# Product-key layers: batch norm's chain moved into layer norm's programs, and four small loads moved ahead

## The reference, cut to what matters

```python
x = x + _L0_ffn_ref(_layernorm(x, axis=-1), gamma, beta, w_q, keys, key_in, key_out)

def _L0_ffn_ref(inputs, gamma, beta, w_q, keys, key_in, key_out):
    x = inputs.reshape(b * n, d)
    mu = jnp.mean(x, axis=0)
    var = jnp.mean(jnp.square(x - mu), axis=0)
    xn = (x - mu) * jax.lax.rsqrt(var + BN_EPS) * gamma + beta
    q = (xn @ w_q.T)...
    sim = jnp.einsum('pbnhd,hkpd->pbnhk', q, keys)
    ...
    o = jnp.einsum('bnd,bnhkd->bnhk', inputs, w_down)
    o = gelu(o) * softmax(scores)
    return jnp.einsum('bnhk,bnhkd->bnd', o, w_up)
```

## Time and profile before

| what | value |
|---|---|
| median of 3 runs | 3775.61 us (3774.59 to 3777.11) |
| the profiled execution's own time | 3767.38 us |
| its span (first to last instruction) | 3765.6 us |
| PE busy | 3243.5 us, 86% |
| DVE busy | 2937.1 us, 78% |
| ACT, POOL busy | 1575.8 us, 42%; 672.2 us, 18% |
| TensorE clock granted, mean | 0.933 of full |
| DMA, mean over the span | 55 GB/s |

### The profile page before, as it was taken

The page is one execution under the profiler, slowest core; times in us unless marked ns, Lnnn a source line. Parts: engine busy times, 40 slices in busy tenths (PEclk is TensorE's granted clock), DMA queues, the critical chain, the costliest instruction groups (busy, mean ns, idle before and its releaser), DMA issues. The chain is left out here.

```text
span 3765.6 us, 81247 instructions
## 1 busy us (share of the span) xinstructions
PE 3243.5 (86%) x29418; PEld 2264.2 (60%) x29418; DVE 2937.1 (78%) x8854; ACT 1575.8 (42%) x2148; POOL 672.2 (18%) x308
## 2 busy tenths in 40 slices
PE   3997579999999985659999999998379999999997
PEld 2886357778787774513333333433357777777786
DVE  5443699999999995458788888860579999999996
ACT  1221244444444431503666666666144444444441
POOL 0000023333333331020000000000013333333333
PEclk6998699999999997857999999999689999999999
DMA  5525500000000002873311333002800000000000
GB/s 175 193 91 159 178 7 10 19 16 13 19 11 19 10 13 88 255 118 49 51 25 32 52 51 52 6 7 67 266 16 10 10 19 11 19 10 19 15 11 15
DMA packets 206472, 207.43 MB, mean 55 GB/s; under 512 B 48694, under 2 KB 182134, under 8 KB 204662
## 3 DMA queue, kind: packets, MB, share of 16 engines
q1 hardware_dynamic: 206070, 202.04, 21.0%
HBM read 129.18 MB, written 72.42 MB: 54 GB/s over the span
## 5 line engine op out<-in xcount | busy, mean ns | idle before, releaser
L514 PE MATMUL f_p_route<-f_x_w,f_y_hot 128*128 128x64 f16 x8192 | 904.6, 194 | 92.2 <-DVE f_weighted L786 71.0
L527 PE MATMUL f_p_hid<-f_xtc,f_kin_t 128*128 128x256 f16 x6144 | 858.4, 274 | 16.9 <-issue 12.1
L538 PE MATMUL f_p_out<-f_kout,f_hidden 128*128 128x256 f16 x6144 | 855.7, 274 | 16.0 <-POOL f_hidden L441 16.0
L441 POOL TENSOR_TENSOR f_hidden<-f_weighted,f_hidden 128x1024 f16<-128x1024 f32 x256 | 610.0, 2383 | 1308.3 <-DVE f_x_w L776 1302.0
L1874 DVE TENSOR_REDUCE at_part_max<-at_p_ring 128x1 f32<-128x512 f32 (+3 forms) x1280 | 696.8, 603 | 139.5 <-PE at_p_ring L1740 69.4
L514 PEld LDWEIGHTS f_p_route<-f_x_w,f_y_hot 128*128 128x128 f16 x8192 | 694.2, 98 | 143.2 <-issue 117.2
L538 PEld LDWEIGHTS f_p_out<-f_kout,f_hidden 128*128 128x128 f16 x6144 | 602.3, 98 | 194.3 <-issue 119.1
L1857 ACT ACTIVATE at_prob<-at_p_s 128x1024 f32<-128x1024 f32 (+3 forms) x640 | 541.3, 895 | 295.5 <-PE at_p_s L1766 168.1
L527 PEld LDWEIGHTS f_p_hid<-f_xtc,f_kin_t 128*128 128x128 f16 x6144 | 602.2, 98 | 94.4 <-issue 25.0
L631 ACT CAST f_hidden<-f_weighted 128x1024 f16<-128x1024 f32 x256 | 342.9, 1339 | 495.5 <-DVE f_weighted L786 495.5
L626 ACT ACTIVATE f_hidden<-f_p_hid 128x512 f32<-128x512 f32 x512 | 302.7, 595 | 517.0 <-PE f_p_hid L527 516.3
(11 more groups left out here) (251 smaller groups left out, 3165.7 us busy)
## 6 DMA issues: line engine op xcount, KB each, us to landing
at_q<-qk SPq DMA_DIRECT2D x48, 256.0 KB, 15.3
at_k<-qk SPq DMA_DIRECT2D x48, 256.0 KB, 17.2
f_ln_xin<-x SPq DMA_DIRECT2D x16, 512.0 KB, 6.6
xt<-f_ln_xt SPq DMA_DIRECT2D x32, 256.0 KB, 5.1
f_kin_t<-kin_t SPq DMA_DIRECT2D x8, 1024.0 KB, 7.9
f_kout<-kout_parts SPq DMA_DIRECT2D x8, 1024.0 KB, 6.9
f_xt_in<-xt SPq DMA_DIRECT2D x32, 256.0 KB, 3.0
f_xres<-x SPq DMA_DIRECT2D x32, 256.0 KB, 2.7
```

The source lines that it names most:

```text
L441: nc.gpsimd.tensor_tensor(lo, weighted[s % WR], hi, ALU.subtract).then_inc(lo_ready, 1)
L514: last = nc.tensor.matmul(p_route[:, t, :], y_hot[:, s % HR, t // PAIR, :, t % PAIR], x_w[:, s % HR, half, t // PAIR, :, t % PAIR], start= ...
L527: last = nc.tensor.matmul(p_hid[g % 2][:, xp % 2, :], kin_t[:, a, dh, xp * P:(xp + 1) * P], xt[slot][:, b, dh, :], start=i % 6 == 0, stop= ...
L538: last = nc.tensor.matmul(p_out[:, u, :], parts[slot][:, xp, u * P:(u + 1) * P, a], kout[:, b, xp, :], start=g == 0 and i == 0, stop=xp == ...
```

## The change

Batch norm's Block is gone. `layer_norm_pass` has three new hooks: `last_loads(sp)` after SP's last prefetch and before its wait for the stores (it first waits for as many landings of the even blocks' stores as block 0 has), `last_root(act)` after ACT's loop, and `last_statistics(dve)` after DVE's loop. DVE's and ACT's parts of batch norm's chain are passed in as the latter two, with the same instructions. Gamma and beta are loaded by `load_ahead` right behind the first prefetch of the first turn. Chunk 0 and the experts' identity are loaded by `last_loads`; their tiles and their two semaphores are allocated ahead of layer norm, as are batch norm's four semaphores. In the experts' Block SP no longer loads the identity and chunk 0.

```diff
@@ layer_norm_pass: sync, after the loop's second turn
                 if prefetch is not None:
                     prefetch(sp, 1, u)
+            if last_loads is not None:
+
+                sp.wait_ge(xt_stored[0], ONE + 16 * NK)
+                last_loads(sp)
             for u in range(2):
                 sp.wait_ge(xt_stored[u], ONE + 16 * NBLK // 2 * NK)
@@ layer_norm_pass: scalar, after the loop
+            if last_root is not None:
+                last_root(act)
@@ layer_norm_pass: vector, after the loop
+            if last_statistics is not None:
+
+                dve.wait_ge(counted, ONE + NBLK)
+                last_statistics(dve)
@@ product_key_memory
         hidden = [sb(f"hidden{i}", [P, NX, CH]) for i in range(2)]
+        ident, xt_in = sb("ident2", [P, P]), sb("xt_in", [P, DH, CH])
 
+        consts_loaded, xt_loaded = sem(tag + "consts_loaded"), sem(tag + "xt2_loaded")
         weights_loaded, kout_loaded = sem(tag + "weights_loaded"), sem(tag + "kout_loaded")
...
-            layer_norm_pass(nc, sem, tag + "ln_", x_dram, xt_dram, ident_dram, bn_st, prefetch=load_weights)
 
             gb_loaded, bn_steps = sem(tag + "gb_loaded"), sem(tag + "bn_steps")
             bn_var_ready, bn_root_ready = sem(tag + "bn_var_ready"), sem(tag + "bn_root_ready")
-            block = first.enter_context(nc.Block())
-
-            @block.sync
-            def _(sp):
-                with nc.allow_non_contiguous_dma(reason="512 scalars"):
-                    sp.dma_start(gb[:, 0, :], gamma.rearrange("(h p) -> p h", p=P)).then_inc(gb_loaded, 16)
-                    sp.dma_start(gb[:, 1, :], beta.rearrange("(h p) -> p h", p=P)).then_inc(gb_loaded, 16)
-
-            @block.scalar
-            def _(act):
+
+            def load_first_chunk(sp):
+                sp.dma_start(xt_in[:], xt_dram[0, :, :, :]).then_inc(xt_loaded, 16)
+                sp.dma_start(ident[:], ident_dram).then_inc(consts_loaded, 16)
+
+            def feature_root(act):
                 act.wait_ge(bn_var_ready, ONE + 1)
                 nc.scalar.activation(scale[:], bn_var[:], ACT.Sqrt).then_inc(bn_root_ready, 1)
 
-            @block.vector
-            def _(dve):
+            def feature_scales(dve):
                 chain = Chain(dve, bn_steps)
...
+            def load_ahead(sp, turn, u):
+                load_weights(sp, turn, u)
+                if (turn, u) == (0, 0):
+                    with nc.allow_non_contiguous_dma(reason="512 scalars"):
+                        sp.dma_start(gb[:, 0, :], gamma.rearrange("(h p) -> p h", p=P)).then_inc(gb_loaded, 16)
+                        sp.dma_start(gb[:, 1, :], beta.rearrange("(h p) -> p h", p=P)).then_inc(gb_loaded, 16)
+
+            layer_norm_pass(nc, sem, tag + "ln_", x_dram, xt_dram, ident_dram, bn_st, prefetch=load_ahead,
+                            last_loads=load_first_chunk, last_root=feature_root, last_statistics=feature_scales)
@@ routed_experts: the two tiles, the two semaphores and the first loads
-        ident = sb("ident2", [P, P])
-        xt_in = sb("xt_in", [P, DH, CH])
-        consts_loaded, iota_ready = sem(tag + "consts_loaded"), sem(tag + "iota_ready")
-        xt_loaded, xn_ready, xt_copied = sem(tag + "xt2_loaded"), sem(tag + "xn_ready"), sem(tag + "xt2_copied")
+        iota_ready = sem(tag + "iota_ready")
+        xn_ready, xt_copied = sem(tag + "xn_ready"), sem(tag + "xt2_copied")
...
-            sp.dma_start(ident[:], ident_dram).then_inc(consts_loaded, 16)
-            load_xt(0)
             load_xt(1)
             rounds(sp, one)
```

More of the change, by code:

```diff
@@ L56, in layer_norm_pass @@
 def layer_norm_pass(nc, sem, tag, x_dram, xt_dram, ident_dram, feature_stats=None, xln_dram=None,
-                    prefetch=None):
+                    prefetch=None, last_loads=None, last_root=None, last_statistics=None):
     with ExitStack() as ctx:
@@ L324, in _, with routed_experts @@
                 chain.link(nc.vector.tensor_tensor(shift[:], gb[:, 1, :], bn_tmp[:], ALU.subtract))
-        routed_experts(nc, sem, tag, x_dram, y_dram, xt_dram, ident_dram, wct, kin_t, kout, scale, shift,
-                       weights_loaded, kout_loaded, hidden)
-def routed_experts(nc, sem, tag, x_dram, y_dram, xt_dram, ident_dram, wct, kin_t, kout, scale, shift, weights_loaded,
-                   kout_loaded, hidden):
+            def load_ahead(sp, turn, u):
[6 more added lines that the diff above has]
+                            last_loads=load_first_chunk, last_root=feature_root, last_statistics=feature_scales)
+        routed_experts(nc, sem, tag, x_dram, y_dram, xt_dram, ident, xt_in, wct, kin_t, kout, scale, shift,
+                       consts_loaded, xt_loaded, weights_loaded, kout_loaded, hidden)
+def routed_experts(nc, sem, tag, x_dram, y_dram, xt_dram, ident, xt_in, wct, kin_t, kout, scale, shift, consts_loaded,
+                   xt_loaded, weights_loaded, kout_loaded, hidden):
     with ExitStack() as ctx:
```

## The result

The changed kernel took 3755.39 us (median of 6 runs, 3744.94 to 3760.60), the kernel before 3774.15 us in runs on the same chip: ratio 0.9947, 95% interval 0.9933 to 0.9961. That is 18.8 us less where 10.7 were forecast. So the two profiles are only 6.8 us apart and cannot show the whole gain.

What follows compares the result with a forecast made beforehand. It took waits between layer norm and the experts' first product as the bound, then chunk 0's landing in the DMA queue. 5.6 + 5.1 = 10.7 us off 3775.61 gave 3764.9 us, range 3759.0 to 3768.8.

Steps and rivals of the forecast that it cites:

- The Block and the chain: Between layer norm and experts: batch norm's 2.6 us chain fits beside SP's wait for the last stores, leaving one barrier.
- the 0.1 us to spare: First layer: the chain ends near 424.95, SP's wait for the stores near 425.05; failing cover costs up to some 0.5 us.
- Chunk 0 behind kout: At layer norm's end: chunk 0 lands 0.9 us behind the last kout load plus 0.4, and its landing releases ACT.
- The next bound: Experts' start: SP's semaphores, `base_ready` among the last, keep ACT from starting before 428.1 (second layer 2728.0), whatever has landed.
- Gamma and beta: Their loads in layer norm's first turn cost nothing, at worst about 1 us per layer.
- The path: ACT's first normalisation starts 5.6 us earlier in the first layer, 5.1 in the second, together 10.7 us.
- Clock at the start: PE's first score products in the experts: no net change from TensorE's clock, 1 us either way in each layer.
- A: Rival: chunk 0 is not held up by kout and SP's semaphores decide; gain 15.5 us, 3760.1 us; chance 0.15.
- B: Rival: chunk 0 pays its whole 2.7 us behind kout, or layer norm grows; gain 7.1 us, 3768.5; chance 0.18.
- D: Rival: the chain on DVE ends well after the stores and ACT waits for scale and shift; 3775 us; chance 0.03.
- C: Rival: slower, the experts' rounds lose the gain to more low-clock stretches; 3793 us at a doubling; chance 0.02.
- the base: Starting time of the sum: 3775.61 us for the kernel before, with 1 to 2 us between two sets of runs.

Runs made afterwards that it cites:

- e3: Changed kernel with chunk 0 and the identity issued ahead of the last kout load, not behind it: 3751.58 us, ratio to before 0.9951.
- e5: Changed kernel with only chunk 0's and the identity's loads moved; batch norm keeps its Block, with gamma and beta loaded there: 3767.05 us, ratio 0.9987.
- e8: Changed kernel with chunk 0 and the identity ahead of the last kout load and `base_ready` allocated first of the experts' semaphores: 3745.01 us, ratio 0.9927.
- e2: The kernel before, run again unaltered: 3769.39 us, ratio 1.0001.
- e9: Changed kernel with a Block that only waits put back where batch norm's was: 3761.80 us, ratio 0.9979.
- e11: Kernel before with eight passed waits ahead of PE's first score product in both layers: 3780.00 us, ratio 1.0035.
- e6: Changed kernel with a pause of eight unread copies of chunk 0 ahead of ACT's first normalisation in both layers: 3765.36 us, ratio 0.9986.
- e12: The changed kernel, run a third time unaltered: 3754.39 us, ratio to before 0.9957.
- e4: Changed kernel with batch norm's chain moved but chunk 0 and the identity loaded in the experts' Block as before: 3758.48 us, ratio 0.9961.
- e10: Changed kernel with eight passed waits ahead of PE's first score product in both layers: 3764.81 us, ratio to before 0.9989.
- e14: Changed kernel with sixteen passed waits ahead of PE's first score product in both layers: 3766.51 us, ratio to before 0.9991.
- e17: Changed kernel with sixteen passed waits ahead of PE's first score product in the second layer alone: 3762.74 us, ratio to before 0.9979.
- e16: Changed kernel with eight passed waits ahead of PE's first score product in the second layer alone: 3753.04 us, ratio to before 0.9952.
- e18: Changed kernel with eight passed waits ahead of PE's first score product in the first layer alone: 3757.09 us, ratio to before 0.9959.

## Why the prediction was wrong, by its own steps

*What was right.* **The Block and the chain:** from the chain's end to the experts' first instruction are 0.56 us in the first layer and 2.30 in the second. In the second the stores end last, as predicted. In the first it is the bare length of a barrier, so the chain was last there and the 0.1 us to spare were not; it cost nothing, since ACT got chunk 0 only 4.7 us after that, the slack that the prediction named. **Chunk 0 behind kout:** 0.6 and 0.7 us behind it, predicted 0.9; released by the DMA, predicted so; e3 shows that the load in front is the cause. **The next bound** behind it, the semaphores with `base_ready`: found in e3 and e5, removed in e8. **Gamma and beta:** no instruction waits for them, layer norm (first load of x to the end of the last statistics) lasts 53.3 us in the first layer of both kernels, and in the second 53.3 in after against 53.7 in before. That 0.4 us goes with the Block, which the forecast did not have: e2, e5, e9 and e11 have 53.7 to 53.8 there, all kernels without a Block 53.2 to 53.3. **The path:** 10.2 us in the profiled pair, 10.8 by the means of the stretches, against 10.7. Part of this closeness is luck: in the second layer kout took 8.0 us to land and not 6.8, and the shorter layer norm and chunk 0's 0.7 for 0.9 took back half of that. **Clock at the start:** the eight score products took 5.89 us instead of 5.13 in the first layer and 6.46 instead of 5.81 in the second, 0.76 and 0.65 us longer, within the 1 us given.

*The rivals.* A (chunk 0 not held up) is refuted by the landings and by e3. B (a whole lone load behind kout) is refuted by the landings: 0.6 and 0.7 us behind it, not 2.7. D did not occur. C alone asked whether anything behind L594 changes, and was priced only as a loss.

*The steps that failed.* Two terms of "3775.61 - 10.7 = 3764.9" were off, by about the same amount. The first is the base. The prediction took the median of three executions and gave the difference of two sets 1 to 2 us; 99 later executions of the same kernel have a mean of 3770.1, 5.5 us lower. With it the forecast is 3759.4, just inside the stated range. The second is a term put at nothing: "all on the path, since everything behind L594 hangs on it and keeps its order", and "the change touches no instruction there". The path gave 10.8 us, the kernel 15.9. Order and instructions are the same, but the time is not: dropping the Block is worth 5.1 us more than the path, and putting an empty one back costs 7.6 (e9). The sum had no term for this and the range no room. So 3764.9 - 5.5 (base) - 5.1 (extra) = 3754.3, against 3754.2 measured over 16 executions.

*How much of this is shown.* That the extra gain of some 5 us is not in the stretch is shown (e6, e12). That it goes with the Block is shown by e5 against e4 and by e9, which gives it and a little more back. Its cause is open. Part is seen: from the last store's issue to the end of the span 4.0 us pass in before and 3.6 in after, 0.4 us that the stretch does not hold. The place of PE's loops is worth 9 to 13 us where they move by 8 instructions and more (e10, e14, e17, and e11 against before), so a cost of this size without a changed step is possible. But the Block moves PE's code by 2 instructions in the first layer and 4 in the second, and a move of the second layer's loop by 4 costs nothing that can be measured (e16, e18). What is left is the first layer's and the attention's place on PE by 2 instructions, the code of DVE, POOL and SP, and the barrier itself; no run separates them, since none had the Block's barrier without its instructions, or its instructions on those engines alone.

## What to carry to other kernels

Work back from the first product behind a stage's start and ask, for each barrier and each load on the way, what it waits for; here that gave the path to within 0.5 us, and doing it once more (chunk 0 ahead of the 1 MB load, the semaphore that is waited for first set up first) gave another 9 us. An edit that adds or removes instructions ahead of a long loop of the bounding engine shifts that loop in its code. Here that moved the time by up to 13 us of 3770 with no step of the work changed, so a forecast below that size needs this in its range, the base should be the mean of many executions and not the median of three, and a measured gain below it needs a control, such as a few passed waits ahead of the loop and the same ones behind it. Take the size of the shift from the profile's count of instructions, not from the source. Look at the loop's turns in the profile: "issue" before a product, and the granted clock of just those stretches.

## What the runs showed of the hardware that had not been expected

- Eight waits that had long passed, four instructions of 0.05 us each in e10's trace, made a kernel 10.6 us (after) and 10 us (before) slower when put ahead of PE's loops in both layers, and nothing when put behind them or on ACT.
- PE's loop of over 1300 products a turn stands still twice at each turn in the second layer, 1.0 to 1.6 and 1.3 to 2.7 us, while four blocks of 16 KB of instructions arrive within some 16 us. In the loop of the second layer a fall to the low clock follows in one turn of three, or in 19 of 20, by where the code lies.
- A semaphore's first increment takes SP 0.06 us: 18 of them 1.06 us in before, 24 of them 1.42 us in after.
- 256 KB behind a 1 MB load in the queue landed 0.6 and 0.7 us after it, 7.2 and 8.0 us after its own issue; alone it takes 2.7. The Trainium skill, in "DMA: Bandwidth & Descriptors", section "Latency and other measured facts", puts the memory's latency at 2 us under high load. No such extra shows behind kout's landing; how much of the 7.2 and 8.0 us is latency and how much queueing, no run separates.
